# Side work of an attention stage handed out in fixed shares, and the last rows spread into its draining steps

## The reference

```python
x = layernorm(x + (softmax(q @ k.T / sqrt(32) + alibi, causal) @ v) @ Wo + bo)   # q, k, v = x @ W + b, 16 heads
logits = x @ Wr + br; top_w, top_idx = top_k(softmax(logits), 1)
y = ((silu(x @ Wg[e]) * (x @ Wu[e])) @ Wd[e])[e == top_idx] * top_w
return layernorm(x + y)
```

## Time and profile before

| what | value |
|---|---|
| median of 3 runs | 1237.4 us (1236.69 to 1239.76) |
| profiled execution, its own time | 1245.01 us |
| its span | 1243.2 us |
| mean granted TensorE clock | 0.961 |
| PE busy / PEld busy | 1149.7 us (92%) / 1028.2 us (83%) |
| DVE / ACT / POOL busy | 728.6 / 589.2 / 520.8 us |

### The profile page before, as it was taken

One profiled execution on the slowest core, in us unless ns is written; L12 is line 12 of the kernel. 1 busy time (PEld: TensorE's weight loads), 2 busy tenths in 40 slices (PEclk: granted clock), 3 DMA queues, 4 the chain that ended last, 5 costly groups with the idle time before them and its releaser, 6 DMA issues.

```text
span 1243.2 us, 25807 instructions
## 1 busy us (share of the span) xinstructions
PE 1149.7 (92%) x7658; PEld 1028.2 (83%) x7658; DVE 728.6 (59%) x1975; ACT 589.2 (47%) x1475; POOL 520.8 (42%) x662
## 2 busy tenths in 40 slices
PE   6999988999899987599999999999999999999994
PEld 5788867887788765498899899889988988998893
DVE  4666676657666744556654663664566366556664
ACT  3687766775787774143332332333233233323354
POOL 6966654754576574423311330331133033113336
PEclk9899999999999987599999999999999999999997
DMA  9233233232233320342132122313313222331302
GB/s 287 53 76 69 63 94 77 53 72 82 69 74 71 94 71 35 119 146 84 54 87 84 52 86 69 85 53 86 86 52 86 69 79 59 86 86 53 86 36 102
DMA packets 105374, 100.10 MB, mean 81 GB/s; under 512 B 10271, under 2 KB 79519, under 8 KB 105248
## 3 DMA queue, kind: packets, MB, share of 16 engines
q1 hardware_dynamic: 100064, 87.18, 26.0%
q0 software_dynamic: 3040, 9.18, 2.2%
q10 hardware_dynamic: 2144, 2.10, 0.6%
HBM read 64.74 MB, written 9.18 MB: 59 GB/s over the span
## 4 chain that ended last, share of the span: by engine, by line
PE 50%; POOL 7%; DMA 3%; issue 2%; ACT 2%; DVE 1%; SPq 0%; ACTq 0%; POOLq 0%; DVEq 0%
PE bank L910 36%; PE bank L935 8%; POOL up_lo L1641 5%; DMA up_raw<-in_Wu_dram 3%; PE bank L922 3%; PE bank L682 1%; ACT up_hi L1065 1%; PE bank L776 1%; PE bank L884 1%; POOL out_dram L1708 1%; POOL pT_lo L1632 0%; DMA y<-x_scratch,row_token 0%; PE bank L872 0%; ACT pT_hi L1042 0%; ACT probs L1035 0%
## 5 line engine op out<-in xcount | busy, mean ns | idle before, releaser
L1641 POOL TENSOR_TENSOR up_lo<-up_raw,up_hi 128x256 fp32r<-128x256 f32 x241 | 171.1, 746 | 483.3 <-ACT up_hi L1065 483.3
L910 PE MATMUL bank<-up_hi,xsT_hi 128*128 x1216 | 356.5, 293 | 9.2 <-POOL up_lo L1641 8.4
L910 PE MATMUL bank<-up_hi,xsT_lo 128*128 x1216 | 344.9, 284 | 0.0
L910 PE MATMUL bank<-up_lo,xsT_hi 128*128 x1216 | 344.7, 284 | 0.0
L1632 POOL TENSOR_TENSOR pT_lo<-probs,pT_hi 128x512 fp32r<-128x512 f32 (+1 forms) x192 | 210.9, 1105 | 139.3 <-ACT pT_hi L1042 138.5
L1456 DVE SCALAR_TENSOR_TENSOR h_tok<-bank,row_weight,silu 128x128 f32<-128x128 f32 x304 | 93.4, 347 | 296.1 <-ACT silu L1150 296.1
L910 PEld LDWEIGHTS bank<-up_hi,xsT_hi 128*128 128x128 f32 x1216 | 233.5, 192 | 16.0 <-issue 15.7
L910 PEld LDWEIGHTS bank<-up_hi,xsT_lo 128*128 128x128 f32 x1216 | 234.3, 193 | 0.3
L910 PEld LDWEIGHTS bank<-up_lo,xsT_hi 128*128 128x128 f32 x1216 | 233.9, 192 | 0.0
L1150 ACT ACTIVATE silu<-bank 128x256 f32<-128x256 f32 (+1 forms) x160 | 59.6, 372 | 365.8 <-PE bank L910 365.8
L1473 DVE TENSOR_TENSOR y<-bank,y 128x512 f32<-128x512 f32 x295 | 198.9, 689 | 0.5
(11 more groups left out here) (181 smaller groups left out, 2087.1 us busy)
## 6 DMA issues: line engine op xcount, KB each, us to landing
stack<-qk SPq DMA_DIRECT2D x180, 128.0 KB, 2.4
up_raw<-in_Wg_dram SPq DMA_DIRECT2D x64, 256.0 KB, 3.4
up_raw<-in_Wu_dram SPq DMA_DIRECT2D x64, 256.0 KB, 4.5
down_raw<-in_Wd_dram SPq DMA_DIRECT2D x64, 256.0 KB, 2.6
x_tok<-in_x_dram SPq DMA_DIRECT2D x16, 256.0 KB, 3.8
x_scratch<-res SPq DMA_DIRECT2D x12, 256.0 KB, 2.4
w_raw<-in_Wo_dram SPq DMA_DIRECT2D x1, 1024.0 KB, 8.7
stack<-max_row SPq DMA_DIRECT2D x64, 2.0 KB
```

The lines of the kernel that those rows point to most:

```text
L910: mm = pe.matmul(bank[:, n * 2 * P:(n + 1) * 2 * P], a[:, s, k, :], up_w[w][k][:, :, :].rearrange("p a f -> p (a f)")[:, bass.ds(at, 2 * P ...
L1641: pool.tensor_tensor(up_w[1][k][:, e, :], up_raw[:, idx % NUPS, k, :, :].rearrange("p g f -> p (g f)"), up_w[0][k][:, e, :].bitcast(F32), ...
```

## The change

The budgets by what is owed go; each half step of a group has a fixed share (`SHARE`, by batch and group, the last entry for the draining steps), raised only when K and Q are due. A share that is overdrawn is taken off the next half step (`over`). The queue is no longer in order: `rank` sorts the jobs that are ready. K and Q of the next group are put off in the third group of batches 1 and 2 while they are far from due, V in the second and fourth group of every batch, and logits come last except in the last batch. All rows of the batch ahead are queued at once when they become ready. The last half step of all only ends a job that has begun. `UP_STEPS` moves by nine steps, and the loads of experts 2 and 3 move behind the loop on SP. A further need keeps an OP behind the turn of the row that used its place in `res`.

```diff
-UP_STEPS = (5, 9)
+UP_STEPS = (14, 18)
+SHARE = ((370,) * GPB, (440, 580, 590, 450), (440, 580, 590, 450), (400, 440, 470, 500), (700,))
-    rows_due, fresh = deque(), []
-    row_counts = (0, 3, 2, 2), (0, 2, 2, 3)
+    fresh = []
+        if kind == "OP":
+            return [("read", "OT", t)] + [("begun", "x1t", t - NX)] * (NX <= t < T0)
-    def work(u, half, budget):
-        while budget > 0 and (left or queue):
+    def work(u, half, share):
+        budget, over = share - over, 0
+        last_half = u == WORK - 1 and half
+        while (left if last_half else budget > 0 and (left or queue)):
             if not left:
-                now_job = next((j for j in queue if all(k in ready for k in needs(j))), None)
+                order = sorted(queue, key=lambda j: rank(u, half, j))
+                now_job = next((j for j in order if all(k in ready for k in needs(j))), None)
...
+        over = max(-budget, 0)
+    def rank(u, half, job):
+        g = min(u // PER_GROUP, NG - 1)
+        if job[0] in ("K", "Q"):
+            later_rows = g % GPB == 2 and 0 < g // GPB < LAST
+            return 3 if later_rows and kq_owed(g, u) / (2 * max(KQ_DUE - u % PER_GROUP, 1) - half) < 0.8 * SHARE[g // GPB][g % GPB] else 1
+        if job[0] == "V" and g % GPB:
+            return (3, 1, 3)[g % GPB - 1]
+        return {"xT": 0, "OT": 0, "x1t": 1, "logit": 1 if g // GPB == LAST else 4}.get(job[0], 2)
+    def kq_owed(g, u):
+        later_kq = 2 * 12 * 213 if u - g * PER_GROUP < KQ_STEP and 0 < g < NG - 1 else 0
+        now = sum(c for _, c in left) if left and now_job[0] in ("K", "Q") else 0
+        return later_kq + now + sum(sum(cost_of(j)) for j in queue if j[0] in ("K", "Q"))
-        if g == NG - 1:
-            return max(owed() / (2 * (WORK - u) - half), 430)
...
-        return max((owed() + later_kq) / (2 * (PER_GROUP - step) - half), due / (2 * max(KQ_DUE - step, 1) - half))
+        due = kq_owed(g, u)
+        return max(SHARE[g // GPB][g % GPB] if u < U else SHARE[NB][0], due / (2 * max(KQ_DUE - step, 1) - half))
...
-                    rows_due.extend((b - 1, n) for n in range(QT + 3))
-                for _ in range(row_counts[b == LAST][m] if b else 0):
-                    queue.extend(row_jobs(*rows_due.popleft()))
+                if m == 1 and b:
+                    for n in range(QT + 3):
+                        queue.extend(row_jobs(b - 1, n))
-                elif m == 2 and 0 < b < LAST:
-                    queue.extend([("K", g + 1), ("Q", g + 1)])
...
-                if u - QT in [U - PER_GROUP + step for step in UP_STEPS]:
-                    load_up(0, UP_STEPS.index(u - QT - U + PER_GROUP) + NUPS)
             assert next_stack == NB * NH
+            for e in range(NUPS, NE):
+                load_up(0, e)
             for t in range(T0, NT):
                 store_x1(t)
```

More of the change, by code:

```diff
@@ L170, in make_plan @@
     ready = {("begun", "OP", -1), ("begun", "logit", -1)} | {("x", b, j) for b in range(2) for j in range(QT)} | {("read",) + job for job in first}
-    queue, left, now_job, pending, later = deque(), [], None, [], deque()
-    rows_due, fresh = deque(), []
-    row_counts = (0, 3, 2, 2), (0, 2, 2, 3)
+    queue, left, now_job, pending, later, over = deque(), [], None, [], deque(), 0
+    fresh = []
     def needs(job):
@@ L184, in needs @@
             return [("o", t // QT * NH + (DONE if t // QT == LAST else NH) - 1), ("begun", "OP", t - 1)]
-        return {"OP": [("read", "OT", t)], "x1t": [("ln", t), ("begun", "logit", t - 1)], "logit": [("read", "x1t", t)], "bv_wo": [("split", kind)]}[kind]
+        if kind == "OP":
+            return [("read", "OT", t)] + [("begun", "x1t", t - NX)] * (NX <= t < T0)
+        return {"x1t": [("ln", t), ("begun", "logit", t - 1)], "logit": [("read", "x1t", t)], "bv_wo": [("split", kind)]}[kind]
     def flush(u):
@@ L196, in flush @@
         pending = []
-    def work(u, half, budget):
-        nonlocal left, now_job
-        while budget > 0 and (left or queue):
+    def work(u, half, share):
+        nonlocal left, now_job, over
+        budget, over = share - over, 0
+        last_half = u == WORK - 1 and half
+        while (left if last_half else budget > 0 and (left or queue)):
             if not left:
-                now_job = next((j for j in queue if all(k in ready for k in needs(j))), None)
+                order = sorted(queue, key=lambda j: rank(u, half, j))
+                now_job = next((j for j in order if all(k in ready for k in needs(j))), None)
                 if now_job is None:
@@ L221, in work @@
                 pending.append(now_job)
-    def owed():
-        return sum(c for _, c in left) + sum(sum(cost_of(j)) for j in queue)
+        over = max(-budget, 0)
[11 more added lines that the diff above has]
+        return later_kq + now + sum(sum(cost_of(j)) for j in queue if j[0] in ("K", "Q"))
     next_x, turned = 0, []
@@ L305, in make_plan @@
         fresh.clear()
[L306 to L309, removed]
+    assert not later and not left
     plan.after_loop = []
```

## The result

The changed kernel takes 1232.34 us (median of 10 executions, 1228.92 to 1238.95) where the kernel before takes 1241.61 us in its ten (1236.69 to 1245.63): ratio 0.9936 over all executions, 95% interval 0.9917 to 0.9956 (the two medians alone give 0.9925). By that ratio it is faster by some 8 us; the forecast was 16. Its profiled execution took 1232.5 us (span 1230.7). In the changed kernel most lines moved by eleven: the score matmul is line 799, `OT`/`OP`/projections' matmul 693, the turned values 848, the normalising 1294, the mask 1323.

A forecast was written before the change was run, and what follows sets the result against it. PE bounds the kernel, with gains where it idles or runs at its lower clock. Terms -16.4 - 5.0 - 1.1 + 0.9 + 1.3 + 4.3 = -16.0 give 1229.0 profiled, 1221.4 us by the median; range 1211 to 1237.

The forecast's parts named there:

- Batches 1 and 2: Steps 66 to 85 and 114 to 133: evenly spread side jobs save 7.5 and 8.9, together 16.4 us.
- rival in which the rows' chain keeps its pace: Rows' jobs follow each other through two banks whatever the share; total only -3.2, 1234.2 us; chance 0.24.
- all of the excess goes: Spread jobs leave neither PE waits nor lower clock; batches 1 and 2 save 25.0, total 1212.9 us; chance 0.13.
- estimate of 21.9: Both rows' stretches: weight loads brought to 88% busy would save 21.9 us instead of 16.4.
- 3.5 us wasted: Batches 1 and 2: PE time the remaining short steps, 70 to 88, still waste under the new plan, against 6.9 before.
- prediction's prices: Attention steps: 0.99 us of PE per step without side work, plus 1.065 us per nominal us of side work.
- factor of 2.2: Batches 1 and 2: excess over wasted time, 15.3 against 6.9 before, assumed to hold for the new plan.
- The sum: Whole kernel: all terms together give -16.0 us, taken off the profiled execution's 1245.0.
- Batch 3: Steps 164 to 191: filling empty steps saves 5.0 us, work leaving for the draining steps 1.1 more.
- Drain: Draining steps: splits of experts 0 and 1 moved there cost +1.3 us (0 to 6.3).
- Tail: Behind the last head: `OP` 14, `OT` 15 and `OP` 15 left over cost +4.3 us (2.1 to 6.4).
- Batch 0: Share of 370 delays K of group 4 and empties one more step: +0.9 us (0 to 1.7).

The follow-up runs named there:

- e12: The changed kernel with VectorE normalising behind the mask and bias instead of ahead, `x1t` where the change has it: 1224.76 us, ratio 0.9878.
- e3: The changed kernel with the `x1t` of rows 8 to 11 ready for planning one step later: 1231.71 us, ratio 0.9905.
- e9: The changed kernel with `x1t` one step later, drain share 1100 instead of 700, and VectorE normalising behind mask and bias: 1219.11 us, ratio 0.9809.
- e2: The kernel before with fixed shares in batch 3 and the drain only, up weights moved: 1246.53 us, ratio 1.0027.
- again: A second profiled execution of the unchanged kernel before: 1240.79 us, ratio 0.9985.
- e4: The kernel before with only the up weights moved (splits at steps 194 and 198, loads behind the loop): 1238.90 us, ratio 0.9973.
- e6: The changed kernel with `x1t` of rows 8 to 11 one step later and a drain share of 640 instead of 700: 1231.62 us, ratio 0.9907.
- e1: The kernel before with fixed shares in batches 0 to 2 only; batch 3, drain and up weights as before: 1230.83 us, ratio 0.9915.
- e5: The kernel before with fixed shares in batches 0 to 2 only, and the up weights moved as in the change: 1228.06 us, ratio 0.9886.
- e7: The changed kernel with `x1t` of rows 8 to 11 one step later and a drain share of 1100 instead of 700: 1227.72 us, ratio 0.9882.

## Why the prediction was right and wrong

**Batches 1 and 2: right in mechanism, in size partly by luck.** The term was 16.4, from 55.7 and 57.1 us to 48.2 each; the stretches take 47.8 and 48.4 from step to step. As forecast, step 81 has side work, step 84 is at the upper level and the waits on `pvT` fall. The rival in which the rows' chain keeps its pace (6.8 saved here) falls, and so does that in which all of the excess goes (its sum adds up to 1211.9, not 1212.9). The Trainium skill (Perfetto Trace Analysis, section Identifying the Most-Contended Engine) says to judge TensorE's headroom by the weight loads' busy share, from which the prediction had an estimate of 21.9. The trace does not bear that out: the share rose to 76% (36.52 of 47.90 us), not to 88%.

Two slips of the count cancel here. `make_plan` puts 20.2 us nominal into each stretch and not 19.4, 0.9 us more; and of the 3.5 us wasted, 0.6 lies behind the stretch, in steps 86 to 88. By the prediction's prices 20 x 0.99 + 20.2 x 1.065 = 41.3 us are needed, so the stretches are 6.5 and 7.1 over at 3.0 wasted: the factor of 2.2 held. But the uneven shares alone do not make it: with VectorE's order changed (e12) the same plan is 4.9 over.

**Its reference: off by 3 us.** The sum was made against one execution. The second one of before has 3 us less in these stretches; by that the term is 13.

**Batch 3: the step that failed.** The prediction put it so: the old excess is 9.7 over 9.2 of wasted time, "at a little more, 1.3, 4.7 is left and 5.0 saved", and 1.1 of work leaves. Instead of 59.6 - 6.1 = 53.5 the stretch took 60.3 us. Its plan was nearly right: `OP` 9 to 11 come one step earlier than by hand, and step 190 stays empty. What failed is the factor: it priced steps by how much side work PE has, and let the takes' waits scale with that. By the prediction's prices the stretch needs 27 x 0.99 + 21.96 x 1.065 = 50.1 us; it is 10.2 over at 2.5 wasted, a factor of 4 and not 1.3. Two waits that hang on where the normalising stands make the difference: an `x1t` first in the next step (e3), and the mask behind the normalising (e9, e12). At the upper clock level the first costs 2.4 us (e12 against e9) and the second 3.4 (e3 against e9). Without both the stretch takes 53.5 us, 3.4 over at 3.0 wasted, a factor of 1.1. The changed kernel's profiled execution also has the clock at 0.58 there, and e2 and e12, with the same wait, do not; up to 3.4 us of the 60.3 may be that execution's (8.1 us at 0.58 instead of 1.00).

That e9 meets the forecast's 53.5 is luck in part, since the counts behind it were off. The 59.6 us of the earlier trace rows hold 27 steps and not the 28 that the 49.9 is made of, so the old excess was 10.7. And the stretch's work does not fall by 1.07 nominal but rises by as much, from 20.9 to 22.0: `x1t` 11 and logit 11 leave it, but the second half of `V` 7 slides into it from steps 156 to 158. With the plan's own counts, 50.1 and 1.3 times 2.5 give 53.4, so the slips cancel.

**Drain: sign wrong, small.** The sum had +1.3; it took 1.1 (again: 2.7) less. I charged ScalarE's splits to the drain and gave nothing back for the steps that they left; e4 shows that the move gains 0.1 to 0.45% by itself. ScalarE never waits for `up_raw` there, as forecast.

**Tail: mechanism right, one job too many.** +4.3 was forecast for three jobs, +2.3 came with two, since `OP` 14 still found its place. e6, with the three, has +3.3, so the price was 1.0 too high.

**Batch 0:** +0.9 forecast, +0.7 (again: +2.0) measured. The experts, which nothing touches, differ by up to 4.4 us between the profiled executions in the table; that is not explained here.

With batch 3's term at +1.0 (steps 144 to 190, first profile) instead of -6.1, the rest of the sum as forecast would give -8.9; the ratio says -8. That they are so close is luck too: against the second profile the drain and the tail came 4.0 and 2.0 better than the sum had them, batches 1 and 2 3.3 worse, and batch 0, batch 3 and the experts some 1 each. That the gain lies in batches 1 and 2 is shown by e1, that the fixed shares behind them lose by e5 against the changed kernel. Of the two causes in batch 3, VectorE's order is shown by the traces and by whole times (e9 against e7, e12 against the changed kernel); `x1t` right behind its normalising is shown by the traces of e2, e3, e9 and e12, while in whole times e3 overlaps the changed kernel.

## What to carry to other kernels

When side work is spread evenly over TensorE, price each step on every engine's queue: an elementwise operation that only side work needs belongs behind what the main pipeline waits for, and a consumer should not be planned first in the step behind its producer. An excess factor from one stretch carries to another only if the same waits make it up. Count the steps and the work of a stretch in the plan itself, and make the sum against two profiled executions, not one.

## What the runs showed of the hardware

**VectorE's normalising waits for GpSimd.** A `tensor_scalar` of 128x512 float32 in SBUF took 0.54 to 0.55 us where no `pT_lo` ran beside it. Of the changed kernel's twelve, the six that began within 0.16 us behind a `pT_lo` of 512 columns took 1.41 to 1.52 us; a quarter of the columns took 1.21 to 1.33 in the same places. The whole ones end 0.28 to 0.29 us behind `pT_lo`, the quarters 0.08 to 0.09; and where it begins 0.98 us behind the start of `pT_lo` (e9 and e12, step 181), it again ends 0.28 behind. The Trainium skill (SBUF — State Buffer, section Who interferes with whom) states such a rule: VectorE and GpSimd share a pair of ports, the instruction that comes first holds it to its end, and the other, which can be a `tensor_scalar`, is blocked and not slowed. These runs agree with it; the prediction did not weigh it.

**The lower clock comes and goes with the same plan.** Steps 86 to 89 have the same side work in the changed kernel and in e7. They take 8.6 us in the one and 12.2 in the other, where the clock is at the lower level although PE is busy throughout. Step 85 ahead of them takes 4.46 us in both, with PE waiting 2.2 us; what lowered the clock in one of them alone is not shown. The first window is the changed kernel's:

```profile
205.00:215.20 10.20, 9.73 (x63) 7.89 (x62) 7.71 (x28) 8.44 (x20) 5.24 (x8) 1.00 0.18 39
```

and this one e7's, from the same steps on:

```profile
206.60:216.80 10.20, 10.20 (x43) 8.86 (x42) 5.84 (x19) 7.04 (x16) 4.36 (x5) 0.50 0.18 39
```

At the upper level nearly all steps of one plan agree within 0.05 us between executions; what these differ by in the attention stage is mostly such stretches.
